# A fused attention and feed-forward kernel: in pass two the gate's columns share the product of the merged experts, made in two halves, and the context comes transposed from the host

## What is computed

```
x = x + L0_xattn(layernorm(x), ctx, ctx)     # autocorrelation attention by Fourier transforms
x = x + L0_ffn(layernorm(x))                 # one linear layer with eight merged adapters
x = x + L1_xattn(layernorm(x), ctx, ctx)     # attention, 32 query heads, 8 key and value heads
x = x + L1_ffn(layernorm(x))                 # the block of experts, below
# L1_ffn(h):
logits = h @ gate_w                          # 8 columns; routing weights: the two highest
shared = relu(h @ up_w) ** 2 @ down_w        # 512 -> 1024 -> 512
routed = ((h @ fc1_w) @ expert_w) * sum(two highest logits) @ fc2_w
out = layernorm(shared + routed) * gamma + beta
```

## Time and profile before

| | us |
|---|---|
| median of 3 runs | 775.92 (775.92 to 775.98) |
| the profiled execution | 776.95 |
| its span, first to last instruction | 775.1 |
| mean granted clock of TensorE | 0.971 |

### The profile page before, as it was taken

The page is one execution under the profiler, slowest core; times in us unless marked ns, Lnnn a source line. Parts: engine busy times, 40 slices in busy tenths (PEclk is TensorE's granted clock), DMA queues, the critical chain, the costliest instruction groups (busy, mean ns, idle before and its releaser), DMA issues.

```text
span 775.1 us, 12226 instructions
## 1 busy us (share of the span) xinstructions
PE 708.1 (91%) x3824; PEld 487.6 (63%) x3824; DVE 473.3 (61%) x1136; ACT 492.4 (64%) x865; POOL 362.7 (47%) x446
## 2 busy tenths in 40 slices
PE   3888999999988468899999999999999999999894
PEld 2334445544444346677877777777778778777673
DVE  1567768787771555656666666665765765765412
ACT  2466666575641786786786786786786786786210
POOL 1165785465553331444454454444544534635323
PEclk9999999999999678999999999999999999999997
DMA  8354322232221311101101001011011011000000
GB/s 279 104 110 137 136 82 82 87 105 70 81 68 69 112 55 41 41 2 55 34 22 55 28 26 54 10 44 41 14 54 41 14 54 41 27 14 27 1 14 28
DMA packets 26086, 45.69 MB, mean 59 GB/s; under 512 B 3233, under 2 KB 5025, under 8 KB 26049
## 3 DMA queue, kind: packets, MB, share of 16 engines
q1 hardware_dynamic: 26048, 45.24, 18.6%
HBM read 36.84 MB, written 8.39 MB: 58 GB/s over the span
## 4 chain that ended last, share of the span: by engine, by line
PE 79%; ACT 5%; POOL 4%; issue 4%; DVE 4%; DMA 2%; SPq 1%; POOLq 0%; DVEq 0%; ACTq 0%
PE ps_b L977 7%; PE ps_b L979 7%; PE ps_b L978 7%; PE wide L1083 6%; PE wide L977 4%; PE wide L978 4%; PE wide L979 4%; PE ps_b L1161 3%; PE bank L1055 3%; PE wide L1045 3%; PE ps_a L1023 3%; PE ps_b L1023 3%; PE bank L977 2%; PE ps_a L977 2%; PE ps_a L978 2%
## 5 line engine op out<-in xcount | busy, mean ns | idle before, releaser
L597 POOL TENSOR_TENSOR va<-mv,small 128x1 f32<-128x1 f32 x80 | 15.3, 191 | 205.5 <-DVE mv L957 98.4
L408 ACT ACTIVATE q_stack<-qt_h 32x512 fp32r<-32x512 f32 x128 | 80.6, 630 | 1.9
L1083 PE MATMUL wide<-w_m,x1t 128*128 128x512 f32 x128 | 60.8, 619 | 0.7 <-ACT x1t L429 0.7
L977 PE MATMUL ps_b<-down_h,ht_h 128*128 128x512 f32 x128 | 53.7, 419 | 4.8 <-DVE ht_l L881 3.4
L889 DVE RECIPROCAL y<-ps_b 128x256 f32<-128x256 f32 x32 | 56.0, 1751 | 0.0
L686 POOL TENSOR_TENSOR y_l<-y,y_h 128x512 fp32r<-128x512 f32 x16 | 20.6, 1289 | 72.9 <-ACT y_h L541 72.9
L977 PE MATMUL wide<-up_h,t_h 128*128 128x512 f32 x128 | 53.0, 414 | 1.1 <-DVE t_l L868 1.1
L672 POOL TENSOR_TENSOR kbd_b<-kt_h,small 128x512 bf16<-128x512 f32 x32 | 34.2, 1093 | 37.8 <-ACT kt_h L510 37.8
L912 DVE TENSOR_TENSOR x<-ps_b,x_res 128x512 f32<-128x512 f32 x16 | 11.1, 692 | 66.8 <-PE ps_b L979 66.8
L978 PE MATMUL wide<-up_l,t_h 128*128 128x512 f32 x128 | 51.2, 400 | 0.0
L979 PE MATMUL wide<-up_h,t_l 128*128 128x512 f32 x128 | 51.2, 400 | 0.0
(11 more groups left out here) (184 smaller groups left out, 2088.7 us busy)
## 6 DMA issues: line engine op xcount, KB each, us to landing
ctx_t<-in_ctx SPq DMA_DIRECT2D x32, 256.0 KB, 2.8
x_in<-in_x SPq DMA_DIRECT2D x16, 256.0 KB, 2.7
x_res<-in_x SPq DMA_DIRECT2D x16, 256.0 KB, 2.7
x_in<-x_rows SPq DMA_DIRECT2D x16, 256.0 KB, 2.6
x_res<-x_rows SPq DMA_DIRECT2D x16, 256.0 KB, 3.5
out<-stage SPq DMA_DIRECT2D x16, 256.0 KB, 2.0
stage<-in_L_ffn_up_w SPq DMA_DIRECT2D x2, 1024.0 KB, 5.2
x_rows<-x SPq DMA_DIRECT2D x8, 256.0 KB, 2.6
```

The costliest lines, as they stand in the source:

```text
L408: last = act.activation(out[STACK * part:STACK * (part + 1), p, :], halves[STACK * p:STACK * (p + 1), :].bitcast(F32), ACT.Copy)
L977: pe.matmul(out_ps, w_hi, m_hi, start=start, stop=False)
L1083: last = pe.matmul(bank[7], cols(x1t, c, P), cols(w0_m, c, D), start=(c == 0), stop=(c == DC - 1))
```

## The change

1. The host passes the context a second time, transposed within each tile. Pass two loads this instead, TensorE no longer transposes it, and ScalarE and VectorE read the tile in SBUF and not a bank of PSUM when they make c_h and c_l. Where SyncE waited for the transposes before the next load, it waits for c_l. TensorE's wait for ct_lo ahead of the second half of the up product goes, since bank 7 isn't shared any more.
2. The eight columns of the gate stand beside the 512 of the merged experts in rt_h and rt_l. The product of 520 columns is made in two halves: columns 256 to 519 into bank 4, then columns 0 to 255 into the right half of bank 2, the latter behind a wait for x3_s. The eight small matmuls and the reduction of their two parts are gone.
3. VectorE takes the maxima and rw out of the first half, and later in its order: behind the second ht_l, ahead of xn4. ScalarE makes routed in two activations, behind a further wait for kv_s.

```diff
-        rt_h, rt_l = sb("rt_h", [P, DC * D], F32R), sb("rt_l", [P, DC * D], F32R)
-        gate_hl = sb("gate_hl", [P, DC, 2, EXPERTS], F32R)
+        rt_h, rt_l = sb("rt_h", [P, DC, D + EXPERTS], F32R), sb("rt_l", [P, DC, D + EXPERTS], F32R)
...
# SyncE, load2
-                    wait(sp, S["ct_ps"], t)
-                    sp.dma_start(ctx2[:], rows(ctx_rows, t)).then_inc(S["ctx2_loaded"], 16)
+                    wait(sp, S["ct_lo"], t)
+                    sp.dma_start(ctx2[:], rows(turned_rows, t)).then_inc(S["ctx2_loaded"], 16)
...
# ScalarE, context_high
-                    act.wait_ge(S["ct_ps"], t + 1)
+                    act.wait_ge(S["ctx2_loaded"], 16 * (t + 1))
                     wait(act, S["kv_ps"], t)
-                    act.activation(ct_h[:], turned_bank(t, True), ACT.Copy).then_inc(S["ct_hi"], 1)
+                    act.activation(ct_h[:], ctx2[:], ACT.Copy).then_inc(S["ct_hi"], 1)
...
# ScalarE, routed, t = i + 1
-                    act.wait_ge(S["rt_out_ps"], t + 1)
+                    act.wait_ge(S["rt_out_ps"], 2 * t + 2)
+                    wait(act, S["kv_s"], capped(1, t + 4))
                     act.wait_ge(S["rw_s"], t + 1)
                     wait(act, S["z_s"], t)
-                    act.activation(routed[:], bank[4], ACT.Copy, scale=rw[:]).then_inc(S["routed_s"], 1)
+                    act.activation(routed[:, HALF:], bank[4][:, 0:HALF], ACT.Copy, scale=rw[:])
+                    act.activation(routed[:, 0:HALF], bank[2][:, HALF:], ACT.Copy, scale=rw[:]).then_inc(S["routed_s"], 1)
...
# VectorE, context_low
-                    dve.tensor_tensor(ct_l[:], turned_bank(t, True), ct_h[:].bitcast(F32), ALU.subtract
+                    dve.tensor_tensor(ct_l[:], ctx2[:], ct_h[:].bitcast(F32), ALU.subtract
...
# VectorE, t = i + 1: taken from behind xn3
-                    dve.wait_ge(S["gate_ps"], t + 1)
-                    dve.tensor_reduce(logits[:], bank[4][:, 0:2 * EXPERTS].rearrange("p (a e) -> p e a", a=2),
-                                      AX.X, ALU.add).then_inc(S["lg_s"], 1)
-                    wait_alone(dve, S["lg_s"], t + 1, S["x_loaded"], 16)
-                    dve.max(lg[:], logits[:]).then_inc(S["top_s"], 1)
...
# and put behind the second ht_l, ahead of xn4
+                    wait_alone(dve, S["rt_out_ps"], 2 * t + 1, S["x_loaded"], 16)
+                    dve.max(lg[:], bank[4][:, HALF:HALF + EXPERTS]).then_inc(S["top_s"], 1)
+                    dve.wait_ge(S["top_s"], t + 1)
+                    wait(dve, S["routed_s"], t)
+                    dve.tensor_tensor(rw[:], lg[:, 0:1], lg[:, 1:2], ALU.add).then_inc(S["rw_s"], 1)
...
# TensorE
-            def turn_context(t):
...
-                    for c in range(DC):
-                        last = pe.transpose(cols(turned_bank(t, True), c, P), cols(ctx2, c, P), ident)
-                    last.then_inc(S["ct_ps"], 1)
...
                     for n in range(2):
-                        if n == 1:
-                            wait(pe, S["ct_lo"], capped(1, t + 4))
...
-                    for c in range(DC):
-                        pe.matmul(bank[4][:, 0:2 * EXPERTS], cols(t4_h, c, P),
-                                  gate_hl[:, c].rearrange("p a e -> p (a e)"), start=(c == 0), stop=False,
-                                  skip_group_check=True)
-                        last = pe.matmul(bank[4][:, 0:EXPERTS], cols(t4_l, c, P), gate_hl[:, c, 0, :],
-                                         start=False, stop=(c == DC - 1), skip_group_check=True)
-                    last.then_inc(S["gate_ps"], 1)
...
-                    pe.wait_ge(S["lg_s"], t + 1)
-                    for c in range(DC):
-                        last = split_product(bank[4], cols(t4_h, c, P), cols(t4_l, c, P),
-                                             cols(rt_h, c, D), cols(rt_l, c, D), c == 0, c == DC - 1)
-                    last.then_inc(S["rt_out_ps"], 1)
+                    for lo, hi, out_ps in ((HALF, D + EXPERTS, bank[4]), (0, HALF, bank[2][:, HALF:])):
+                        if lo == 0:
+                            wait(pe, S["x3_s"], capped(1, t + 2))
+                        for c in range(DC):
+                            last = split_product(out_ps[:, 0:hi - lo], cols(t4_h, c, P), cols(t4_l, c, P),
+                                                 rt_h[:, c, lo:hi], rt_l[:, c, lo:hi], c == 0, c == DC - 1)
+                        last.then_inc(S["rt_out_ps"], 1)
...
# host
+    laid["ctx_turned"] = _np.asarray(inputs["ctx_4096"]).reshape(NT, P, DC, P).transpose(0, 3, 2, 1)
```

More of the change, by code:

```diff
@@ L27 @@
 EPS = 1e-5
+HALF = D // 2
 Q0, K0, V0, W0, DFT = 0, P, 2 * P, 3 * P, 4 * P
@@ L108, in build @@
     ctx_rows = ctx_in.rearrange("b s d -> (b s) d")
+    turned_rows = ctx_tr.rearrange("t p c n -> (t p) (c n)")
     out_rows = out.rearrange("b s d -> (b s) d")
@@ L225, in build @@
             bn3_s mv3_s va3_s rs3_s xn3_s bn4_s mv4_s va4_s rs4_s xn4_s bn5_s mv5_s va5_s rs5_s zn_s
-            ct_ps ct_hi ct_lo kv_ps kv_s qx_ps qx_hi qx_lo qy_ps q_s
+            ct_hi ct_lo kv_ps kv_s qx_ps qx_hi qx_lo qy_ps q_s
             sel_in sel_s qs_s kp_s qkt_ps kt_hi kt_lo qt_hi qt_lo qt_bs kbd_s vbd_s g_ps gmax_s gmt_ps ngm_s s_ps probs_s
             pv_ps den_s y_s y_hi y_lo wo_ps x2b_s x3_s x3b_s x3c_s
-            t4_ps t4_hi t4_lo u_ps relu_s h_s gate_ps lg_s top_s rw_s rt_out_ps routed_s
+            t4_ps t4_hi t4_lo u_ps relu_s h_s top_s rw_s rt_out_ps routed_s
             ht_ps ht_hi ht_lo dn_ps z_s zg_s o_s
@@ L265, in early, with turned_bank, capped @@
             return isinstance(i, int) and i == EARLY + later
-        def turned_bank(t, bank_of_ctx):
-            first_tile = isinstance(t, int) and t == 0
-            return bank[(3 if first_tile else 7) if bank_of_ctx else (4 if first_tile else 5)]
+        def turned_bank(t):
+            return bank[4 if isinstance(t, int) and t == 0 else 5]
         def down_staged(i):
             return isinstance(i, int) and i < 3 - LEAD2
+        def capped(n, t):
+            return n * (min(max(t, 0), NT) if isinstance(t, int) else t)
         def pass2_loop(eng, body, peeled=lambda i: None):
@@ L494, in peeled @@
                         act.wait_ge(S["rt_ps"], c + 1)
-                        act.activation(rt_h[:, c * D:(c + 1) * D], bank[6 + c % 2], ACT.Copy).then_inc(S["rt_hi"], 1)
+                        act.activation(rt_h[:, c, 0:D], bank[6 + c % 2], ACT.Copy).then_inc(S["rt_hi"], 1)
             pass1_loop(body, peeled)
@@ L503, in body2 @@
                     act.wait_ge(S["t4_ps"], t + 1)
-                    wait(act, S["rt_out_ps"], t)
+                    wait(act, S["rt_out_ps"], 2 * t)
                     act.activation(t4_h[:], bank[4], ACT.Copy).then_inc(S["t4_hi"], 1)
@@ L866, in body2 @@
                     dve.wait_ge(S["t4_hi"], t + 1)
-                    wait(dve, S["rt_out_ps"], t)
+                    wait(dve, S["rt_out_ps"], 2 * t)
                     dve.tensor_tensor(t4_l[:], bank[4], t4_h[:].bitcast(F32), ALU.subtract).then_inc(S["t4_lo"], 1)
@@ L983, in _ @@
             pe.wait_ge(S["dft_loaded"], 16)
-            def turn_context(t):
-                if live(t):
-                    pe.wait_ge(S["ctx2_loaded"], 16 * (t + 1))
-                    wait(pe, S["probs_s"], 2 * (t - 1))
-                    if isinstance(t, int) and t == 0:
-                        pe.wait_ge(S["vsw_s"], NT)
-                        pe.wait_ge(S["shift_s"], NT)
-                    for c in range(DC):
-                        last = pe.transpose(cols(turned_bank(t, True), c, P), cols(ctx2, c, P), ident)
-                    last.then_inc(S["ct_ps"], 1)
             def keys_values(t):
@@ L1006, in keys_values @@
                     for c in range(DC):
-                        last = pe.transpose(cols(turned_bank(t, False), c, P), cols(xn3, c, P), ident)
+                        last = pe.transpose(cols(turned_bank(t), c, P), cols(xn3, c, P), ident)
                     last.then_inc(S["qx_ps"], 1)
@@ L1034, in body @@
                     transform(ps_b, K0, ctx_t).then_inc(S["k_ps"], 1)
-                if early(i):
-                    turn_context(0)
                 t = i
@@ L1121, in _ @@
             pe.wait_ge(S["stage_lo"], 2 * len(WEIGHTS))
-            def capped(n, t):
-                return n * (min(max(t, 0), NT) if isinstance(t, int) else t)
             def body2(i):
```

26 lines of the change are left out of this document (11 added, 15 removed).

## The result

The changed kernel takes **780.66 us** (780.52 to 781.03) against 775.95 of the kernel before on the same chip (775.92 to 776.38): a ratio of 1.0059 with a 95% interval of 1.0044 to 1.0074, so 4.7 us slower. The profiled execution took 780.79, its span is 779.0 and the mean granted clock 0.962, where before had 775.1 and 0.971. The two medians lie further apart (4.7) than the two spans (3.9), because the profiled execution of before was 1.0 over its median and that of after only 0.1.

The account below looks back on a forecast made before the run. The loop of waits through y, with 0.42 us slack, was taken as the bound: +4.9 (loop) -1.5 (pass one's end) +1.0 (fill) -0.6 (first full period) -2.0 (drain) = +1.8, so 777.7 us; range 769.5 to 782.

Parts of the forecast that it names:

- the largest of the three chances: Whole kernel: slower was given 0.46, faster 0.31 and the same 0.23.
- the forecast's own case: Whole kernel: 777.7 us, its own range 775.3 to 780, chance 0.58.
- What bounds the kernel: Pass two: a loop through four engines to y; the down product's wait for y_s has 0.42 us of slack.
- c_l is held by kbd_b: VectorE, pass two: GpSimd's kbd_b holds c_l, ending it 0.68 later; rival not held, 769.8 us, chance 0.16.
- The held rw: VectorE: an addition with both inputs in SBUF, median 160 ns, took 0.80 inside GpSimd's y_l; evidence for the hold.
- Period: Steady pass two: 0.26 later down product, 0.11 restart, 0.07 halves, +0.44 us a period; +4.9 over eleven.
- Halves: Merged product in 264 and 256 columns: +0.07 a period; rival, 264 not at full rate, 782 at +0.4, chance 0.06.
- Iteration -1 of the fill: Start of pass two: wo already waits 0.81 for y_l, so c_l's delay passes on, +0.5 us.
- The rival of the clock: Full iterations: TensorE's clock falls in the new idle time, +1.4 a period eleven times, 793 us; chance 0.06.
- Iteration -2: Fill, the iteration before -1: +0.5 us, half of the fill's +1.0.
- End of pass one: TensorE's wait for the first context and its transposes go; weights' transposes start at 224.19 not 225.68, -1.5 us.
- First full iteration and drain: First full period: hold absent, -0.6 us; drain: three gates go, less halves and waits for routed, -2.0 us.

Follow-up runs that it names:

- gate_only: Against the kernel before: only the gate's columns in the merged product and its halves, context still transposed by TensorE; 771.95 us, ratio 0.993.
- before_cl_sbuf: The kernel before with only VectorE's c_l reading the untransposed context in SBUF instead of PSUM, all matmuls kept; 783.59 us, ratio 1.0075.
- after_cl_psum: The changed kernel with c_l reading PSUM bank 7 again, comparing instead of subtracting, and its up-product wait restored; 774.62 us, ratio 0.9961 to the kernel before.
- warm: The changed kernel plus ten matmuls that compute nothing, in the idle time ahead of wo in iteration -1; 777.95 us, ratio 1.0011 to the kernel before.
- both_late: The changed kernel with c_l moved behind y's products on VectorE and c_h behind y_h on ScalarE; 760.49 us, ratio 0.9772 to the kernel before.
- ctx_only: The kernel before with only the context loaded transposed and read in SBUF by both engines, gate and merged product as before; 782.15 us, ratio 1.0054.
- cl_late: The changed kernel with c_l alone moved behind the products of y in VectorE's order; 767.76 us, ratio 0.9869 to the kernel before.

## Why the prediction was right, and where it was wrong

The forecast was 777.7 with a range of 769.5 to 782; the time is 780.66, so it lies in the range, slower, as the largest of the three chances (0.46) said, but 0.7 above the 775.3 to 780 that the forecast's own case was given. The mechanism in the loop was right. Outside it the errors partly cancelled, which was luck: iteration -1 +3.2, the rest of the fill -0.5, the end of pass one -1.1, the loop +0.3, the drain +0.2, together the 2.1 by which the spans were missed, and 0.9 from the span to the median.

- **What bounds the kernel.** Right: the wait of the down product for y had 0.42 of slack, and gate_only used it up (0.4 idle each time, with 0.88 taken out).
- **c_l is held by kbd_b.** Right, by before_cl_sbuf and after_cl_psum. The delay of y behind the last scores was forecast at 0.68; it is (582.64 - 570.86) - (578.14 - 567.02) = 0.66. The remainder behind the release was taken as 0.55 and is 0.54. The Trainium skill ("SBUF — State Buffer", Who interferes with whom) says that the operation issued first blocks the other fully; of the blocking every run agrees, but of the 0.69 only 0.54 follows the release. The held rw shows it too: it ends at 593.15, 0.02 behind the square's end at 593.13, though alone it takes 0.16.
- **Period.** +0.47 for +0.44, but two parts of it cancel. The release takes 0.15 (582.64 to 582.79) and not the 0.06 that I read off GpSimd's y_l: +0.09. The restart, for which I added 0.11, costs nothing: the down product takes 585.68 - 582.79 = 2.89 behind its idle 1.50, and 2.88 without one. wo's 2.99 has another reason than the wait, since in warm, with no idle time ahead of it, it is 2.99 too: bf16 rough scores follow it, and they start 0.33 behind its last matmul (318.88 to 319.21 in before) where the next product would start after 0.23. So 0.26 + 0.11 + 0.07 was really 0.33 + 0.00 + 0.07, and 0.07 more, some 0.01 to 0.03 in each of several products.
- **Halves.** 592.52 - 589.55 = 2.97 against 2.90, +0.07 as forecast. 264 columns are of full rate; that rival is out.
- **Iteration -1 of the fill.** Wrong by 3.2. The step that failed: "the wo product waits already for y_l, 0.81, so the gate's 0.88 gives nothing there and c_l's delay passes on: +0.5". The +0.46 came; but the time of the gate and the transposes became idle time ahead of wo, and the sum had no term for the clock there. It was asked about only for the full iterations, where it never fell (1.00 from 340 to 680). The rival of the clock had the right mechanism in the wrong place, and its price in the right one is 3.1 (warm). Nor was it right on what decides: it looked for a second idle stretch near the first, and the only other idle time that the profile marks in this iteration ahead of the 2.58 is 0.17, nine us earlier. That the longer idle time is what brought the clock down isn't shown either: before_cl_sbuf keeps the gate and the transposes and idles only 1.27 there, and its wo product takes 322.47 - 317.92 = 4.55 and its iteration -1 30.58 all the same; gate_only idles 1.60 and keeps the full clock. What brings the fall on stays open.
- **Iteration -2.** +0.5 was expected and 0.0 came. Here c_l was issued ahead of the second kbd_b, and the hold fell on GpSimd:

```profile
277.41 0.73 DVE L737 TENSOR_TENSOR c_l<-ctx_t,c_h 128x512 fp32r<-128x512 f32 x1
```

```profile
275.72 3.33 POOL L678 TENSOR_TENSOR kbd_b<-kt_h,small 128x512 bf16<-128x512 f32 x2 [16.35 <-ACT kt_h L514]
```

The two operations of kbd_b take 3.33, where the same two took 2.88 in this iteration of before (0.82 over 2.06, beside down_l, a long VectorE subtraction with both inputs in SBUF that had begun ahead of them). The rough scores wait for kbd_b, but y, and with it wo, does not.
- **End of pass one.** -1.5 was right for its step: from the transposes of the weights before to these is 224.77 - 215.74 = 9.03 instead of 225.68 - 215.17 = 10.51, -1.48, of which 0.57 is not seen in the cut since this execution was that much later before. What I had left out is the last product of pass one: 8 matmuls took 5.40 and take 3.70. After, then before:

```profile
244.02 3.70 PE L1073 MATMUL wide<-w_m,x1t 128*128 128x512 f32 x8 [0.69 <-ACT x1t L433]
```

```profile
244.93 5.40 PE L1083 MATMUL wide<-w_m,x1t 128*128 128x512 f32 x8 [0.69 <-ACT x1t L429]
```

  The idle time ahead of it is 0.69 in both. From 246 to 248 the granted clock is 1.00 in after and 0.50 in before (after first):

```profile
246.00:248.00 2.00, 1.72 (x5) 0.41 (x3) 0.00 (x0) 0.24 (x1) 0.90 (x1) 1.00 0.11 42
```

```profile
246.00:248.00 2.00, 2.00 (x4) 0.85 (x3) 0.00 (x0) 0.00 (x0) 1.73 (x2) 0.50 0.34 131
```

  In all the runs with the turned context it is 3.70, in all those without (gate_only and before_cl_sbuf among them) 5.40; why the clock holds in the one and not in the other isn't settled.
- **First full iteration and drain.** -0.54 for -0.6, and -1.8 for -2.0: right. The longest wait for routed in the drain grew from 1.68 to 1.83, and a new one of 0.22 came up, as the two activations end 0.84 behind the start of the first where the single one took 0.69.
- **From span to median.** I took the 1.0 off by which before's profiled execution exceeded its median; after's exceeds it by 0.1. That is 0.9 of the 3.0 by which the median was missed.

## What to carry to other kernels

Moving an operand from PSUM to SBUF isn't free for the engine that reads it: where VectorE then has both inputs in SBUF and GpSimd is at work, look at what GpSimd executes at that moment and what stands behind the VectorE instruction in its queue. Work taken off the busiest engine pays only as far as the slack in the loop of waits beside it goes (0.22 came back of the 0.88 taken out in gate_only), and in full only once that loop is cut; here two steps that nobody waited for stood ahead of y and y_h, and moving them behind turned +0.6% into -2.3%. In this fill, idle time of TensorE was not neutral (6.3 us over three iterations): price the products behind each idle stretch at the clock that the chip may grant there, and try matmuls that compute nothing in it.

## What the runs showed of the hardware that was not expected

- The length of an idle stretch alone does not tell whether TensorE's clock falls behind it. Ahead of wo in iteration -1 it stayed full behind 1.60 (gate_only) and 1.52 (both_late), and fell behind 1.27 (before_cl_sbuf), 1.79 (ctx_only), 1.96 (cl_late), 2.12 (after_cl_psum) and 2.58 (after). Idle 1.50 once a period, eleven times over, never brought it down. Each of these figures but two is from one execution (after and both_late were traced twice and came out the same), and executions of before on the same chips lie between 775.2 and 779.8 at mean clocks of 0.962 to 0.973, so some of this may differ from one execution to the next.
- A second fall mostly followed a first one, but not only then: the idle 2.49 ahead of the scores cost nothing in before and in gate_only, and with an earlier fall in the same iteration the lowest clock of a stretch of two us behind it was 0.50 in after, after_cl_psum, before_cl_sbuf and cl_late and 0.54 in ctx_only. In both_late it fell there without one in that iteration (0.50 from 326 to 328), so this is no rule.
- The hold works in either direction, by who is issued first: kbd_b grew from 2.06 to 2.88 beside down_l, which the trace of before could have told, and to 3.33 with c_l ahead of its second half. And a held operation doesn't need its whole time behind the end of the holder: c_l needs 0.54 of its 0.69 and rw 0.02 of its 0.16, some 0.15 less in both; xn4 needs 0.29 of its 0.54.
